# Layer 1 of a two-layer attention and expert kernel: the mix scaled on ScalarE, the sine part of the rotation on VectorE, gathers without copies, the kv mask ahead of a combine

## The reference, cut to what matters

```python
# layer 1, xn = layernorm(x)
q, k, v = split(xn @ W_qkv)                    # 16 heads of 16
q, k = q * cos + rotate_half(q) * sin, k * cos + rotate_half(k) * sin
q_feat, k_feat = elu(q * SCALE) + 1, elu(k) + 1
kv = k_feat.T @ v                              # per head
att = (q_feat @ kv) / max(q_feat @ k_sum, 1e-6) @ W_out
xr = mu_r * xn + (1 - mu_r) * x_prev           # x_prev: xn one token earlier
xk = mu_k * xn + (1 - mu_k) * x_prev
gate = sigmoid(xr @ W_r) * (square(relu(xk @ W_k)) @ W_v)
out = x + att + gate
```

## Time and profile before

| | |
|---|---|
| median of 3 runs | 1028.23 us (1025.26 to 1028.94) |
| the profiled execution: its time, its span | 1027.16 us, 1025.5 us |
| busy in the span: PE, PEld, DVE, ACT, POOL | 922.5, 855.2, 756.4, 566.0, 271.4 us |
| mean granted TensorE clock | 0.951 of full |

### The profile page before, as it was taken

One profiled execution on the slowest core, in us unless ns is written; L12 is line 12 of the kernel. 1 busy time (PEld: TensorE's weight loads), 2 busy tenths in 40 slices (PEclk: granted clock), 3 DMA queues, 4 the chain that ended last, 5 costly groups with the idle time before them and its releaser, 6 DMA issues. The chain is left out here.

```text
span 1025.5 us, 19190 instructions
## 1 busy us (share of the span) xinstructions
PE 922.5 (90%) x6533; PEld 855.2 (83%) x6533; DVE 756.4 (74%) x1407; ACT 566.0 (55%) x1123; POOL 271.4 (26%) x308
## 2 busy tenths in 40 slices
PE   3899999989999999999999999984674986989976
PEld 3688999989999999999999999983463856868765
DVE  7685556478888888888888888855953584587843
ACT  3543443356677776667777666755552373466560
POOL 1005666200000000000000000017775636540621
PEclk8999999999999999999999999997895997899988
DMA  8772333459666666666666666513032102100101
GB/s 272 267 242 88 109 123 109 139 188 314 207 207 225 227 227 229 214 205 208 225 226 226 231 213 205 194 42 87 1 90 75 42 1 82 42 0 0 42 1 41
DMA packets 103765, 150.36 MB, mean 147 GB/s; under 512 B 8432, under 2 KB 86832, under 8 KB 103600
## 3 DMA queue, kind: packets, MB, share of 16 engines
q1 hardware_dynamic: 94544, 123.13, 36.5%
q0 software_dynamic: 9184, 26.75, 7.4%
HBM read 112.63 MB, written 37.22 MB: 146 GB/s over the span
## 5 line engine op out<-in xcount | busy, mean ns | idle before, releaser
L960 ACT ACTIVATE h<-ps,b1T 128x256 f32<-128x256 f32 x312 | 129.4, 465 | 139.9 <-PE ps L895 139.7
L893 PE MATMUL ps<-w2h,hh 128*128 128x256 f32 x624 | 179.8, 288 | 0.3 <-DVE hl L1014 0.3
L893 PE MATMUL ps<-xTh,w1h 128*128 128x256 f32 x624 | 177.4, 284 | 1.4 <-DVE xTl L997 1.4
L894 PE MATMUL ps<-xTl,w1h 128*128 128x256 f32 x624 | 177.3, 284 | 0.0
L895 PE MATMUL ps<-xTh,w1l 128*128 128x256 f32 x624 | 177.2, 284 | 0.0
L895 PE MATMUL ps<-w2h,hl 128*128 128x256 f32 x624 | 176.6, 283 | 0.0
L894 PE MATMUL ps<-w2l,hh 128*128 128x256 f32 x624 | 176.5, 283 | 0.0
L878 POOL DMA_DIRECT2D expert_out<-y x38 | 27.2, 717 | 461.0 <-DVE y L1031 461.0
L1014 DVE TENSOR_TENSOR hl<-h,hh 128x512 fp32r<-128x512 f32 x156 | 107.6, 690 | 52.1 <-ACT hh L964 50.4
L893 PEld LDWEIGHTS ps<-xTh,w1h 128*128 128x128 f32 x624 | 120.5, 193 | 1.6 <-DVE xTl L997 1.6
L894 PEld LDWEIGHTS ps<-xTl,w1h 128*128 128x128 f32 x624 | 120.6, 193 | 0.0
(11 more groups left out here) (228 smaller groups left out, 2236.1 us busy)
## 6 DMA issues: line engine op xcount, KB each, us to landing
raw<-in_L_ffn_W SPq DMA_DIRECT2D x40, 1024.0 KB
raw_odd<-in_L_ffn_W SPq DMA_DIRECT2D x38, 1024.0 KB, 8.4
dispatched<-shared SPq DMA_DIRECT2D x1, 9984.0 KB, 34.9
rows<-dispatched SPq DMA_DIRECT2D x39, 256.0 KB, 6.1
expert_out<-y POOLq DMA_DIRECT2D x38, 256.0 KB, 6.9
xn_rows<-raw SPq DMA_DIRECT2D x4, 1024.0 KB, 5.2
rows<-xn_rows SPq DMA_DIRECT2D x32, 128.0 KB
out<-x_acc SPq DMA_DIRECT2D x4, 1024.0 KB, 4.4
```

What stands on the lines that cost most here:

```text
L893: pe.matmul(out, ah, bh, start=start, stop=False, skip_group_check=True)
L894: pe.matmul(out, ah, bl, start=False, stop=False, skip_group_check=True)
L960: op = act.activation(h32[:, k, :], ps[:, q, (k % 2) * M:(k % 2 + 1) * M], ACT.Relu, bias=s.b1T[:, ds(e * HC + k, 1)])
```

## The change

- **Mix.** ScalarE's new `scaled` writes mu times xn into xkT and xrT (four passes of 1024 columns), and VectorE's `mix` adds (1 - mu) times x_prev. GpSimd's `step_T` goes. `act_k` gets a buffer of its own. In sequences 1 to 3 `scaled` stands ahead of ScalarE's qkv copies and both mixes ahead of VectorE's first rotation; in sequence 0 `scaled` stands behind the copies and feature of the second pair, both mixes behind `feature(1)`.
- **Rotation.** The two sine halves move from GpSimd to VectorE, between the cosine pass and the sum.
- **Gathers.** They read the slot numbers directly, with no copy and no wait for it. The first eight gathers go ahead of three memsets. GpSimd has no rotation left, so gathers follow at once where the slots are free.
- **Order on VectorE.** The mask comes behind combine(b+1, 0); combine(b+1, 1) comes behind the mask and the first scales in sequences 1 and 2, and behind divisions 0 and 1 in sequence 0.
- **Order on ScalarE.** The sigmoids come before the squares, with a wait for `final` of the sequence before (gate is written there); the wait for `r_mixed` ahead of relu goes. In sequence 0, `normed(1, 1)` moves between the oT copies.
- **End.** In sequence 3 GpSimd adds the gate to x before the projection is added, VectorE's add is the last, and SyncE stores four pieces of 256 KB. SyncE's loop over the sequences is written out.

```diff
 def gather(pool, s, expert_out, b, i):
     t = b * s.BT + i
-    pool.tensor_copy(s.slot_now[:, i, :], s.slots[:, s.K * t:s.K * t + s.K]).then_inc(s.slot_staged, 1)
-    pool.wait_ge(s.slot_staged, t + 1)
     for k in range(s.K):
+        slot = s.slots[:, s.K * t + k:s.K * t + k + 1]
         pool.indirect_dma_start(out=s.picked_rows[:, i, k, :], out_offset=None, in_=expert_out,
-                                in_offset=bass.IndirectOffsetOnAxis(ap=s.slot_now[:, i, k:k + 1], axis=0)
-                                ).then_inc(s.gathered[i], 16)
+                                in_offset=bass.IndirectOffsetOnAxis(ap=slot, axis=0)).then_inc(s.gathered[i], 16)
...
 # GpSimd
-            def rotate(b):
...
-                        pool.tensor_tensor(step_T[:, :, :], xnT[:, :, 1:T + 1], xnT[:, :, 0:T], ALU.subtract
...
             def finish(b):
                 for n in range(NG):
+                    if b == B - 1:
+                        pool.wait_ge(gated, NG * b + n + 1)
+                        pool.tensor_tensor(x_tile(b * BT + 2 * n, 2), x_tile(b * BT + 2 * n, 2),
+                                           gate[:, 2 * n:2 * n + 2, :].rearrange("p j d -> p (j d)"), ALU.add
+                                           ).then_inc(gate_added, 1)
+                        continue
...
             for b in range(B):
-                rotate(b)
-                for ahead in ((1, 2) if b == 0 else (b + 2,)):
-                    if ahead < B:
-                        gather_sequence(ahead)
+                if b == 0:
+                    gather_some(1, range(BT))
+                if b + 2 < B:
+                    gather_some(b + 2, range(BT))
                 finish(b)
...
 # ScalarE
+            def scaled(b):
+                act.wait_ge(xnT_ready, all_turned(b))
+                for dst, m, done in ((xkT, 1, k_scaled), (xrT, 0, r_scaled)):
+                    for c in range(DC):
+                        op = act.activation(dst[:, c, :], xnT[:, c, 1:T + 1], ACT.Identity, scale=mu[:, m, c:c + 1])
+                    op.then_inc(done, 1)
...
+                if not first:
+                    act.wait_ge(nd_mm, NG * b)
+                    scaled(b)
                 for n in range(NG):
...
+                    if first and n == 1:
+                        act.wait_ge(loaded, 16 * LOADS)
+                        scaled(b)
...
-                act.wait_ge(r_mixed, b + 1)
                 relu(0)
                 features(NG - 1)
                 for n in range(1, 4):
                     relu(n)
-                for n in range(4):
-                    square(n)
-                act.wait_ge(rotated, NG * b + NG)
+                if not first:
+                    act.wait_ge(final, NG * b)
                 for n in range(NG):
                     act.wait_ge(r_mm, NG * b + n + 1)
...
+                for n in range(4):
+                    square(n)
...
 # VectorE
-                def mix(dst, m, done):
+                def mix(dst, m, scaled, done):
+                    dve.wait_ge(scaled, b + 1)
                     for c in range(DC):
-                        op = V.scalar_tensor_tensor(dst[:, c, :], step_T[:, c, :], mu[:, m, c:c + 1], xnT[:, c, 0:T],
-                                                    ALU.mult, ALU.add)
+                        op = V.scalar_tensor_tensor(dst[:, c, :], xnT[:, c, 0:T], rest_of_mu[:, m, c:c + 1],
+                                                    dst[:, c, :], ALU.mult, ALU.add)
...
                                     ALU.mult).then_inc(straight_done, 1)
+                    src = qk[:, n % 2].rearrange("p j (h f) -> p j h f", f=HD)
+                    dst = rot[:, n % 2].rearrange("p j (h f) -> p j h f", f=HD)
+                    for half in range(2):
+                        to = slice(half * HD // 2, (half + 1) * HD // 2)
+                        fro = slice((1 - half) * HD // 2, (2 - half) * HD // 2)
+                        table = sin[:, 2 * n:2 * n + 2, to].unsqueeze(2).to_broadcast([P, 2, 2 * D // HD, HD // 2])
+                        op = V.tensor_tensor(dst[:, :, :, to], src[:, :, :, fro], table, ALU.mult)
+                    op.then_inc(rotated, 1)
...
                 if not last:
                     combine(b + 1, 0)
-                    combine(b + 1, 1)
                 dve.wait_ge(kv_mm, b + 1)
...
                 if not last:
                     scales(b + 1, 0)
+                    if not first:
+                        combine(b + 1, 1)
                 apply_gate(0)
                 apply_gate(1)
-                if not last:
+                if not last and not first:
                     scales(b + 1, 1)
                 divide(0)
                 divide(1)
+                if first:
+                    combine(b + 1, 1)
+                    scales(b + 1, 1)
...
+                    if last:
+                        dve.wait_ge(gate_added, n + 1)
                     V.tensor_tensor(x_tile(b * BT + 2 * n, 2), x_tile(b * BT + 2 * n, 2), ps[:, 4 + n, :], ALU.add
-                                    ).then_inc(out_added, 1)
+                                    ).then_inc(last_final if last else out_added, 1)
...
 # SyncE, last sequence
+            for n in range(NG):
+                sp.wait_ge(last_final, n + 1)
+                sp.dma_start(rows_out[b][:, 2 * n:2 * n + 2], x_tile(b * BT + 2 * n, 2).rearrange(
+                    "p (i d) -> p i d", d=D)).then_inc(stored, 16)
```

More of the change, by code:

```diff
@@ L1065, in combine_and_layer1 @@
         oT = sb("oT", [P, DC, T])
-        qT, act_k = xkT, step_T
+        qT = xkT
         gate = sb("gate", [P, BT, D])
@@ L1137, in _, with gather_some @@
             sp.dma_start(sin[:, :, :], rope_sin.rearrange("(i p) f -> p i f", p=P)).then_inc(loaded, 16)
-            with sp.Fori(0, B) as b:
+            rows_out = out.rearrange("b (i p) d -> b p i d", p=P)
+            for b in range(B - 1):
                 sp.wait_ge(final, NG * b + NG)
-                sp.dma_start(out.rearrange("b (i p) d -> b p i d", p=P)[b],
-                             x_tile(b * BT, BT).rearrange("p (i d) -> p i d", d=D)).then_inc(stored, 16)
-            sp.wait_ge(stored, 16 * B)
+                sp.dma_start(rows_out[b], x_tile(b * BT, BT).rearrange("p (i d) -> p i d", d=D)).then_inc(stored, 16)
+            b = B - 1
+            for n in range(NG):
+                sp.wait_ge(last_final, n + 1)
+                sp.dma_start(rows_out[b][:, 2 * n:2 * n + 2], x_tile(b * BT + 2 * n, 2).rearrange(
+                    "p (i d) -> p i d", d=D)).then_inc(stored, 16)
+            sp.wait_ge(stored, 16 * (B - 1 + NG))
         @block.gpsimd
         def _(pool):
-            def gather_sequence(b):
+            def gather_some(b, tiles):
                 for start, size, count in units(b - 1):
-                    pool.wait_ge(combined, count)
+                    if start in tiles:
+                        pool.wait_ge(combined, count)
                     for i in range(start, start + size):
-                        gather(pool, s, expert_out, b, i)
+                        if i in tiles:
+                            gather(pool, s, expert_out, b, i)
+            for i in range(BT // 2):
+                gather(pool, s, expert_out, 0, i)
             pool.memset(same_head[:, :], 1.0).then_inc(const_ready, 1)
@@ L1450, in body @@
                     normed(b + 1, 0)
-                    normed(b + 1, 1)
+                    if not first:
+                        normed(b + 1, 1)
                 for m in range(4):
                     h, c = m // 2, m % 2
+                    if first and m == 2:
+                        normed(b + 1, 1)
                     act.wait_ge(att_turned, 4 * b + m + 1)
@@ L1550, in body @@
                 if not first:
-                    dve.wait_ge(step_ready, b + 1)
-                    mix(xkT, 1, k_mixed)
+                    mix(xkT, 1, k_scaled, k_mixed)
+                    mix(xrT, 0, r_scaled, r_mixed)
                 turn_by_position(0)
@@ L1555, in body @@
                     turned_lo(0, 3)
-                else:
-                    mix(xrT, 0, r_mixed)
                 for n in range(1, NG):
@@ L1560, in body @@
                     feature(n - 1)
-                    if first and n == 1:
-                        dve.wait_ge(step_ready, b + 1)
-                        mix(xkT, 1, k_mixed)
-                        mix(xrT, 0, r_mixed)
+                    if first and n == 2:
+                        mix(xkT, 1, k_scaled, k_mixed)
+                        mix(xrT, 0, r_scaled, r_mixed)
                 feature(NG - 1)
```

29 lines of the change are left out of this document (8 added, 21 removed).

## The result

The changed kernel takes 1009.74 us (median of 4 runs, 1008.41 to 1010.35) against 1028.45 for the kernel before on the same chip (4 runs, 1025.26 to 1028.94): ratio 0.9823, 95% interval 0.98 to 0.9845. It is faster by 18.7 us, not by the forecast 42, and lies above the range of 973 to 1003. The profiled run is the fastest one, 1008.41 us, with a span of 1006.7 us.

The account below looks back on a forecast made before the run. From each sequence's start to kv the VectorE-ScalarE chain of rotation and features was the limit, then VectorE up to att_ready(2). 17.5 + 8.9 + 3.4 + 11.7 = 41.5 us from 1027.16 gives 985.7, stated as 986; range 973 to 1003.

Parts of the forecast that it names:

- sequence 0's burst: Sequence 0: GpSimd, free of the rotation, gathers sequence 1 from about 711 to 735 instead of starting at 741.88.
- 27.7 us up to 764.92: Sequence 0, TensorE from k's start at 739.5: needs 27.7 us, where it used to idle 7.48 for the mask.
- I am wrong if TensorE waits during sequence 0's qkv products: Sign against the forecast: TensorE waiting in sequence 0's qkv products, or ScalarE's copies holding it.
- The 17.5 us: Sequence 0's forecast gain: mask done early, rows landed, divide(0) at 766.8 instead of 789.71, sequence 1 at 789.9.
- The rival "slower": Stall follows every gather; sequence 1's burst moves into sequence 0's qkv products, costing 24 us; total 1030; chance 0.03.
- two half bursts would cost 10 each: Part of the slower rival: sequence 0's two half bursts of gathers would each cost 10 us.
- Sequence 1, 8.9 forecast: Sequence 1 gains 8.9 us if the stall lasts to the gather burst's end, 17.3 if it is gone.
- The den clip that was to tell the cases apart: Sequence 1, VectorE: some 2 us after the last gather if the stall stays, +47 us by the skill's rule.
- no stall in sequence 1: Rival: sequence 1 loses its stall, 8.4 us more gained, total 978; chance 0.22.
- Sequence 2, 3.4 forecast: Sequence 2: feature(3) 5.5 us earlier, 6.7 won at kv, 3.1 left at att_ready(2), out projection 3.4 earlier.
- Sequence 3, 11.7 forecast: Sequence 3: whole kv gain arrives, 8.2 us, plus tail of 1.3 (GpSimd's add) and 2.3 (smaller last store).
- Partial gain by dearer VectorE: Rival: strided sine halves and scaling cost more than priced, sequence 0 keeps ten of 17.5; total 1010; chance 0.13.

Follow-up runs that it names:

- i2: Changed kernel with sequence 1's sixteen gathers replaced by plain loads of consecutive rows issued by GpSimd: 988.72 us, one run.
- i3: Changed kernel with sequence 1's sixteen gathers replaced by plain loads of consecutive rows issued by SyncE: 987.59 us, one run.
- h1: Changed kernel, sequence 1's gathers held until sequence 0's last qkv product; in sequence 0 k mixed behind feature(0), r behind feature(1): 983.96 us, ratio 0.9622.
- g1: Changed kernel with combine(b+1, 1) back directly behind combine(b+1, 0), ahead of the kv mask: 1009.06 us, ratio 0.985.
- i1: Changed kernel with earlier sequence 0 mix, both combines ahead of the mask, each sequence's gathers issued one sequence before, after its last qkv product: 971.88 us, ratio 0.9477.
- e3: Changed kernel with sequence 1's sixteen gathers replaced by plain loads of 128 consecutive rows issued by SyncE, on chip 13: 976.76 us, one run.

## Why the prediction was wrong, point by point

- **The step that failed is sequence 0's burst.** "GpSimd, free of the rotation, gathers sequence 1 from about 711 to 735" was right to 2 us at its end, and was costed at nothing: TensorE's "27.7 us up to 764.92" and the qkv products before it were taken as they stood. Between the first chip and chip 8 the new order's sequence 0 differs by 22.1 us, and on chip 7 the gap costs 19.5 to 21.4. The stall was priced for sequence 1, where the trace had shown one, and not for the burst that the change moved beside the qkv products, where ScalarE and VectorE wait for a result of TensorE's every few us. The prediction had named this sign itself ("I am wrong if TensorE waits during sequence 0's qkv products"). For the first chip -15.2 (the old stall goes) - 1.3 (the reorder) + 22.1 = +5.6; the three terms come from the same four windows, so this sum is a split of the time and no proof of it. Without the new gap the forecast holds on a stalling chip: i2 and i3 have spans of 987.0 and 985.5, and 1025.5 - 41.5 is 984. That it is so close is partly luck: sequences 0 and 1 are 1 to 3 us longer there than forecast, and sequences 2 and 3 shorter.
- **The reason that was wrong in it.** The 17.5 us were credited to the mask's place and the earlier rows. The new times were right where nothing stalls: on chip 8 k starts at 739.13 (forecast 739.5), divide(0) at 767.31 (766.8), sequence 1 at 790.97 (789.9). The old time was what misled: some 15 us of it were the stall of the old burst (15.2 between the two profiled executions, good to some 6), and the chip without it shows 1.3 won in sequence 0.
- **The rival "slower" named the mechanism**: it put the burst in the qkv products at 24 us, and 19.5 to 22 were measured. Its other price, "two half bursts would cost 10 each", was wrong (i2's sequence 0 has them and takes 103.48, 1.7 more than on chip 8), so the whole stayed a gain. It had 0.03; the argument against it (k and r products not slowed beside a burst) was true and said nothing of qkv: h1 shows 24 us of burst beside k and r, from 727.72 to the end of kv at 752.10, for free.
- **Sequence 1, 8.9 forecast, 6.8 measured.** The stall lasts on to the end of the burst as said, and 9.8 of its 13.8 us are left, so 4.0 went where 5.5 were forecast; the rest gave 2.8 (65.52 to 62.75) and not 3.4. The den clip that was to tell the cases apart came at 869.88, 3.8 us after the last gather's end and 56.9 after the start (55.1 forecast). The rival "no stall in sequence 1" said 978, and chip 8 shows 976.7 with no stall; that is luck, for the kernel before takes 1003 there and not 1027, and it is not the new order that took the stall away. The Trainium skill (SBUF — State Buffer, SBUF: two separate sides) says that TensorE never waits for another engine's port; chip 8 agrees, with no such wait in layer 1. On the others a signal is late, and no run shows that a port has part in it.
- **Sequence 2, 3.4 forecast, 4.0 measured.** Rotation and features right to 0.1 us. att_ready(2), the end of the second division, came 48.7 us after the start, not 49.2, because kv ended 0.7 us earlier than worked out (36.2, not 36.9). g1 shows that the moved mask cost 1.95 here. On chip 8 the old sequence takes 67.17 us, at a granted clock of 0.95 instead of 0.97, and the gain is 5.7.
- **Sequence 3, 11.7 forecast, 13.5 measured.** In the tail it is 1.3 + 3.0 instead of 1.3 + 2.3, and kv ended 36.1 us after the start, not 37.0. On chip 8 the gain is 71.58 less 59.74, 11.8: the old kv products take 3.84 us there and took 5.48 on the first chip, where the granted clock was 0.50 from 993 to 996, behind a wait of 2.06 us (2.16 on chip 8, and the clock held; why is open). So 1.6 of the 13.5 were TensorE's clock.
- "Partial gain by dearer VectorE" was at 1010, the measured number, by another cause: no pass was dear.

## What to carry to other kernels

When a row of the trace shows a stall that no engine explains, price it at every place to which the change moves what stood beside it, above all where engines hand results back and forth every few us. Place bursts of gathers by index beside long products that nobody waits for, and keep them so short that they end there (16 gathers, not 24 or 32; but 16 beside the divisions still cost 9.8 us in sequence 1); with the earlier mix and g1's order that took the ratio on stalling chips from 0.98 to 0.94. And time both kernels on a second chip before a gain is put down to a mechanism: 25 us of the old time were the chip's (medians of 1028.45 and 1003.43).

## What the runs showed of the hardware

- On the first chip and on chips 7, 11 and 12, a run of indirect gathers makes TensorE's signals reach the other engines late, and TensorE issues single instructions 0.7 (h1, 758.75 to 759.48) to 2.1 us apart (changed kernel, 858.34 to 860.44). How soon differs: products that ended 7.6 us after the start of a run of eight were seen 3.8 us late (i3: run from 754.38, products until 761.97, VectorE at 765.78), products that ended 11.2 us after the start 8.9 us late (changed kernel), and beside the k and r products nothing was late for 24 us (h1). It is over 1.5 to 3.5 us after the last gather's end. In i1 signals from the gathers to VectorE came within 2.1 us meanwhile. On chips 8 and 13 nothing of this is seen, at the same 0.95 to 0.96 us per gather.
- The two kinds of chip can be told by one more thing in the view of DMA issues: where nothing stalls, gathers have a time to landing; where it stalls, none is found. The same goes for plain loads, SyncE's small ones too (2.8 us for 16 loads of 128 KB in e3, none in i3), while the stores of 1 MB have one on both. The changed kernel at 712 to 722 us on chip 8, then on the first chip:

```profile
raw<-expert_out,slots POOLq DMA_INDIRECT x8, 2.8
```

```profile
raw<-expert_out,slots POOLq DMA_INDIRECT x9
```

- What the chips differ in stays open. Late instruction fetches are not seen in the changed kernel: the first fetch packet after the gap lies at 740.00 to 740.25, after TensorE has resumed (738.61), and on chip 8, without a gap, it follows the product at the same place by 1.2 us (719.5 after 718.33). The Trainium skill (Runtime: NRT & Kernel Launch, Instruction fetch mechanics) says that the cost of fetching on in sequence is mostly hidden; these packets agree.
